# Joint classifier on one core: the logits load and the last store over two DMA queues, 64 partitions each, instead of SP's alone

## The chip, the cores and the metric

The kernel runs on one core of one Trainium2 chip. The metric is the device time of one execution in microseconds; the number given for a kernel is the median over its runs. A profile of one further execution of the kernel before is quoted below.

## The reference, cut to what matters

```python
# logits (512, 64), y_true (512, 100), float32
variables = [softmax(p, axis=-1) for p in split(logits, 4 parts of 16)]
joint = outer product of the four, per row        # (512, 16, 16, 16, 16)
flat = joint.reshape(B, -1)                       # (512, 65536)
num_y_joint = einsum('bj,by->yj', flat, y_true)   # summed over the rows
num_joint = sum(flat, axis=0)
prob_y_joint = clip(maximum(num_y_joint, 1e-6) / maximum(num_joint, 1e-6), 0, 1)
probs = einsum('yj,bj->by', prob_y_joint, flat)   # (512, 100)
```

Two large products over 65,536 joint states: one from rows to states (`num_y_joint`, with a column of ones beside the labels for `num_joint`), one back from states to rows (`probs`).

## The kernel before, in words

The 512 rows lie on 128 partitions, four (KC) to a partition. The four softmax variables are kept unnormalized; variables 2 and 3 make `p23`, variable 1 scales it into the tiles `p` (32 tiles of 128 states, fp16 in a high and a low part), variable 0 goes with the labels into `q` (four groups of four of its values). TensorE forms for each group and tile `numbers` = p^T q (`count`: twelve matmuls, three for each of the four chunks of rows), VectorE turns `numbers` into ratios (`make_ratios`), and TensorE sums `joined` = pt^T r (`join`: twelve matmuls), with `pt` the transposed `p`, made by DMA transposes of SP. There are 128 such steps. After each group ScalarE copies `joined` out (L271) and GpSimd scales and sums it into `acc`.

Each engine has its own instruction stream, in program order; the engines meet at semaphores only.

The start: SP issues the load of the logits into the tile `x` (L156, 128 partitions of 1 KB, semaphore `logits_in`), then the load of the labels (L157, `labels_in`). ScalarE's stream starts with the load of its function table, which the compiler has put ahead of the first Exp (both have line L217). VectorE waits for `logits_in` (L278), then takes the maxima of each variable (L279) and subtracts them (L283, two halves). ScalarE does the Exp of each half (L217). GpSimd makes the first part of `p23` (L186), ScalarE the first `p_hi` (L220), VectorE the first `qf` (L297, which reads the labels), ScalarE the first `q_hi` (L235), and TensorE's first matmul that counts is L481. Until then TensorE runs matmuls on a tile of zeros whose results are not used (`idle_turns`, L478): 14 from the moment the tile is set, 5 more once the first Exp is done (L491), 3 once `whole` is made (L493), 2 once the first `qf` is made (L495).

The end: the last matmuls (L636 to L638) leave the last 100 columns' sums of chunk 3 in two halves. VectorE adds the four last terms to `acc` (L421, `added`). SP stores chunks 0 to 2 of the result (L174, 150 KB) when their sums are complete, and the last chunk (L176, 128 partitions of 400 bytes) when `added` has reached 20. It then waits for both stores (`stored`, `stored_last`, L177 and L178).

Of the kernel before, what the change touches and what calls it, by code (L numbers as in the profile page):

```python
# [31 lines left out]
def joint_classifier(nc: bass.Bass, logits: bass.AP, y_true: bass.AP, probs: bass.AP):  # L32
    ROWS, WIDTH = logits.shape
    CLASSES = y_true.shape[1]
    LANES = 128
    KC = ROWS // LANES
    S = 16
    NV = WIDTH // S
    AG = 4
# [17 lines left out]
    with ctx:  # L57
        def sb(name, shape, dt):
            return ctx.enter_context(nc.sbuf_tensor(name, shape, dt))
# [4 lines left out]
        def sem(name):  # L64
            return ctx.enter_context(nc.semaphore(name))
# [7 lines left out]
        x = sb("x", [LANES, KC * NV, S], FP32)  # L73
# [25 lines left out]
        acc = sb("acc", [LANES, KC, CLASSES], FP32)  # L99
# [4 lines left out]
        logits_in = sem("logits_in")  # L104
# [31 lines left out]
        added = sem("added")  # L136
# [3 lines left out]
        stored_last = sem("stored_last")  # L140
# [6 lines left out]
        def landings(i):  # L147
            return (i // TURN_SEMS + 1) * 32 - (16 if i % TURN_SEMS == 0 else 0)

        def p_count(i):  # L150
            return KC + 2 if i == 0 else KC * (i + 1)


        @block.sync
        def _(sp):
            sp.dma_start(x[:, :, :], logits.rearrange("(p k) (v s) -> p (k v) s", k=KC, s=S)).then_inc(logits_in, 16)  # L156
            sp.dma_start(labels[:, :, 0:CLASSES], y_true.rearrange("(p k) y -> p k y", k=KC)).then_inc(labels_in, 16)  # L157

            def turn(out, src, i):
                return sp.dma_start_transpose(  # L160
                    out[:, i * 2 * TW:(i + 1) * 2 * TW].rearrange("p (c b) -> p c b", b=LANES),
                    src[:, i * 2 * TW:(i + 1) * 2 * TW])

            for i in range(S):
                landed = pt_landed[i % TURN_SEMS]
                if i >= TURN_SEMS:
                    sp.wait_ge(landed, landings(i - TURN_SEMS))
                sp.wait_ge(p_hi_made, p_count(i))
                turn(pt_hi, p_hi, i).then_inc(landed if i else first_landed, 16)
                sp.wait_ge(p_ready, p_count(i))  # L170
                turn(pt_lo, p_lo, i).then_inc(landed, 16)
            out = probs.rearrange("(p k) y -> p k y", k=KC)
            sp.wait_ge(added, KC * AG)
            sp.dma_start(out[:, 0:KC - 1, :], acc[:, 0:KC - 1, :]).then_inc(stored, 16)  # L174
            sp.wait_ge(added, KC * AG + AG)
            sp.dma_start(out[:, KC - 1:KC, :], acc[:, KC - 1:KC, :]).then_inc(stored_last, 16)  # L176
            sp.wait_ge(stored, 16)  # L177
            sp.wait_ge(stored_last, 16)  # L178

        @block.gpsimd  # L180
        def _(pool):
# [29 lines left out]

        @block.scalar
        def _(act):
            for part in range(2):
                v = NV // 2 * (1 - part)
                act.wait_ge(shifted, part + 1)
                act.activation(ek[:, :, v:v + NV // 2, :], ek[:, :, v:v + NV // 2, :], ACT.Exp).then_inc(exps, 1)  # L217

            def p_hi_chunk(i, k):
                return act.activation(p_hi[:, bass.ds(i * (2 * TW), 2 * TW)].rearrange("p (h k n) -> p h k n", h=2, k=KC)[:, :, k, :],  # L220
                                      p23[:, k, :].rearrange("p (h n) -> p h n", n=HALF),
                                      ACT.Copy, scale=v01s[:, k, 1, bass.ds(i, 1)])

            def first_p_hi(i, k):
                p_hi_chunk(i, k).then_inc(p_hi_made, 1)

            def make_p_hi(i):
                for k in range(KC):
                    last = p_hi_chunk(i, k)
                last.then_inc(p_hi_made, KC)  # L230

            def make_first_q_hi(part, k0, k1):

                act.wait_ge(q_made, part)
                act.activation(q_hi[:, k0 * NW:k1 * NW], qf[:, k0 * NW:k1 * NW], ACT.Copy).then_inc(q_hi_made, 1)  # L235

            def make_q_hi(g):

                for k in range(KC):
                    act.wait_ge(q_made, Q_PARTS + (g - 1) * KC + k + 1)  # L240
                    act.activation(q_hi[:, g * QW + k * NW:g * QW + (k + 1) * NW], qf[:, k * NW:(k + 1) * NW],
                                   ACT.Copy).then_inc(q_hi_made, 1)

            act.wait_ge(exps, 2)
            act.activation(v01s[:, :, :, :], ek[:, :, 0:2, :], ACT.Copy, scale=UP).then_inc(v01s_made, 1)
            act.wait_ge(v01s_made, 1)
            act.wait_ge(p23_first, 1)
            first_p_hi(0, 0)
            act.wait_ge(p23_first, 2)
            first_p_hi(0, 1)  # L250
            make_first_q_hi(1, 0, 1)
            first_p_hi(1, 0)
            make_first_q_hi(2, 1, 2)
            first_p_hi(1, 1)
            act.wait_ge(p23_made, 1)
            first_p_hi(0, 2)
            make_first_q_hi(3, 2, 3)
            first_p_hi(0, 3)
            make_first_q_hi(4, 3, 4)
            first_p_hi(1, 2)  # L260
            first_p_hi(1, 3)
            with act.Fori(2, S) as i:
                make_p_hi(i)

            for g in range(1, GROUPS):
                make_q_hi(g)
                if g > 1:
                    act.wait_ge(sum_chain, 3 * (g - 1) - 2)
                for k in range(KC):
                    act.wait_ge(joined_ready, (g - 1) * KC + (k + 1))  # L270
                    act.activation(left[:, k, :, :], joined[k][:, 0:PW].rearrange("p (a y) -> p a y", a=AG),  # L271
                                   ACT.Copy).then_inc(left_made, 1)

        @block.vector
        def _(dve):

            dve.memset(idle[:, :], 0.0).then_inc(idle_set, 1)
            dve.wait_ge(logits_in, 16)  # L278
            dve.tensor_reduce(stat[:, 0, :], x[:, :, :], AX.X, ALU.max).then_inc(dve_chain, 1)  # L279
            dve.wait_ge(dve_chain, 1)  # L280
            for part in range(2):
                v = NV // 2 * (1 - part)
# [381 lines left out]
```

## Time and profile before

| | us |
|---|---|
| median of 3 runs | 534.14 (534.1 to 534.17) |
| the profiled execution, its time | 534.18 |
| the profiled execution, its span from the first to the last instruction | 532.1 |

| engine | busy us | share of the span |
|---|---|---|
| PE (TensorE, matmul) | 527.9 | 99% |
| DVE (VectorE) | 295.9 | 56% |
| ACT (ScalarE) | 41.7 | 8% |
| POOL (GpSimd) | 24.0 | 5% |

The profile names engines PE, PEld (TensorE's weight load), DVE, ACT, POOL and SP; a q behind the name (SPq, ACTq) is that engine's instruction queue, where the issuing of DMAs and the waits are seen. L156 is line 156 of the kernel. Neighbouring matmuls overlap, so a matmul's own duration is longer than the distance to the next one.

### The profile page before, as it was taken

The numbers are of one execution on the slowest core, as the hardware profiler recorded it, in microseconds if no ns is written. First come the engines' busy times: TensorE is split into PE (matmuls) and PEld (weight loads), VectorE is DVE, ScalarE is ACT, GpSimd is POOL, SyncE is SP. The second block draws the span as 40 slices with busy tenths as digits, with TensorE's granted clock in tenths as the row PEclk, the third lists the DMA queues.
The fourth block names the chain that finished last, engine by engine and source line by source line (L and its number), as shares of the span: only waits on it lengthen the run. The fifth ranks groups of instructions, "written<-read, shape, count | busy, mean of one in ns | idle before, by whom it ended". The sixth has DMA issues, their size and how long they took to land.

```text
span 532.1 us, 8634 instructions
## 1 busy us (share of the span) xinstructions
PE 527.9 (99%) x3108; PEld 303.5 (57%) x3108; DVE 295.9 (56%) x764; ACT 41.7 (8%) x96; POOL 24.0 (5%) x22
## 2 busy tenths in 40 slices
PE   8999999999999999999999999999999999999997
PEld 5555555555555555555555555555555555555555
DVE  7986766754685444444466544444446544444446
ACT  7950000000200000000020000000001000000000
POOL 1000000000130000000032000000005000000000
PEclk9999999999999999999999999999999999999999
DMA  2944524220000000000000000000000000000000
GB/s 45 160 80 79 70 51 79 57 43 1 1 0 2 0 0 0 0 0 0 1 0 1 1 0 0 0 0 0 0 0 1 0 1 0 0 0 0 0 2 15
DMA packets 34770, 9.20 MB, mean 17 GB/s; under 512 B 34496, under 2 KB 34752, under 8 KB 34752
## 3 DMA queue, kind: packets, MB, share of 16 engines
q1 hardware_dynamic: 34752, 8.93, 9.4%
q8 instruction: 14, 0.23, 0.2%
q14 instruction: 4, 0.03, 0.0%
HBM read 0.34 MB, written 0.20 MB: 1 GB/s over the span
## 4 chain that ended last, share of the span: by engine, by line
PE 98%; DVE 1%; DMA 0%; ACT 0%; POOL 0%; issue 0%; ACTq 0%
PE joined L462 16%; PE joined L464 16%; PE joined L463 16%; PE numbers L454 16%; PE numbers L455 16%; PE numbers L456 16%; PE numbers L481 1%; PE numbers L484 1%; PE numbers L487 1%; DVE acc L421 0%; DMA x<-in_r_logits_dram 0%; ACT p_hi L220 0%; PE numbers L584 0%; PE numbers L581 0%; PE numbers L580 0%; PE joined L575 0%
## 5 line engine op out<-in xcount | busy, mean ns | idle before, releaser
L464 PE MATMUL joined<-r_hi,pt_lo 128*128 128x400 f16 x504 | 167.6, 332 | 0.0
L463 PE MATMUL joined<-r_lo,pt_hi 128*128 128x400 f16 x504 | 167.6, 332 | 0.0
L462 PE MATMUL joined<-r_hi,pt_hi 128*128 128x400 f16 x504 | 167.5, 332 | 0.0
L454 PE MATMUL numbers<-q_hi,p_hi 128*128 128x404 f16 x492 | 164.8, 335 | 0.0
L456 PE MATMUL numbers<-q_hi,p_lo 128*128 128x404 f16 x492 | 164.0, 333 | 0.0
L455 PE MATMUL numbers<-q_lo,p_hi 128*128 128x404 f16 x492 | 163.9, 333 | 0.0
L341 DVE TENSOR_SCALAR den<-numbers 128x4 f32<-128x4 f32 x128 | 20.6, 161 | 211.2 <-PE numbers L456 211.1
L353 DVE SCALAR_TENSOR_TENSOR r_lo<-ratio,r_hi 128x400 f16<-128x400 f32 x128 | 78.3, 612 | 4.4
L346 DVE SCALAR_TENSOR_TENSOR ratio<-numbers,inv 128x400 f32<-128x400 f32 x128 | 73.5, 574 | 4.4
L463 PEld LDWEIGHTS joined<-r_lo,pt_hi 128*128 (+1 forms) x504 | 49.2, 98 | 36.3
L462 PEld LDWEIGHTS joined<-r_hi,pt_hi 128*128 (+1 forms) x504 | 49.1, 97 | 36.3
L464 PEld LDWEIGHTS joined<-r_hi,pt_lo 128*128 (+1 forms) x504 | 49.3, 98 | 35.9
L455 PEld LDWEIGHTS numbers<-q_lo,p_hi 128*128 (+1 forms) x492 | 48.4, 98 | 35.8
L456 PEld LDWEIGHTS numbers<-q_hi,p_lo 128*128 (+1 forms) x492 | 47.6, 97 | 36.6
L454 PEld LDWEIGHTS numbers<-q_hi,p_hi 128*128 (+1 forms) x492 | 47.9, 97 | 35.9
L351 DVE TENSOR_SCALAR r_hi<-ratio 128x400 f16<-128x400 f32 x128 | 48.9, 382 | 4.4
L271 ACT ACTIVATE left<-joined 128x400 f32<-128x400 f32 x12 | 5.9, 504 | 317.7 <-PE joined L464 317.7
L321 DVE SCALAR_TENSOR_TENSOR p_lo<-p,v01s,p_hi 128x256 f16<-128x256 f32 x64 | 26.8, 478 | 0.0
L220 ACT ACTIVATE p_hi<-p,v01s 128x256 f32 (+1 forms) x64 | 26.1, 499 | 0.3 <-POOL p L186 0.3
L344 DVE RECIPROCAL inv<-den 128x4 f32<-128x4 f32 x128 | 22.8, 178 | 4.4
L199 POOL TENSOR_TENSOR part<-left,v0f 128x1600 f32<-128x1600 f32 x3 | 8.6, 2864 | 277.4 <-ACT left L271 277.4
L297 DVE SCALAR_TENSOR_TENSOR qf<-labels,whole,v01s 128x404 f32<-128x404 f32 x16 | 11.8, 734 | 0.0
(55 smaller groups left out, 84.7 us busy)
## 6 DMA issues: line engine op xcount, KB each, us to landing
pt_hi<-p_hi SPq DMA_TRANSPOSE x16, 3.1
pt_lo<-p_lo SPq DMA_TRANSPOSE x16, 3.2
labels<-in_r_y_true_dram SPq DMA_DIRECT2D x1, 200.0 KB, 2.9
out_dram<-acc SPq DMA_DIRECT2D x1, 150.0 KB, 1.8
x<-in_r_logits_dram SPq DMA_DIRECT2D x1, 128.0 KB, 2.0
out_dram<-acc SPq DMA_DIRECT2D x1, 50.0 KB, 1.5
```

The costliest lines, as they stand in the source:

```text
L220: return act.activation(p_hi[:, bass.ds(i * (2 * TW), 2 * TW)].rearrange("p (h k n) -> p h k n", h=2, k=KC)[:, :, k, :], p23[:, k, :].rear ...
L321: return dve.scalar_tensor_tensor(lo[:, :, k, :], p23[:, k, :].rearrange("p (h n) -> p h n", n=HALF), v01s[:, k, 1, bass.ds(i, 1)], hi[:, ...
L344: dve.reciprocal(inv[:, slot, :], den[:, slot, :]).then_inc(inv_made, 1)
L346: dve.scalar_tensor_tensor(ratio[:, slot, :].rearrange("p (a y) -> p a y", a=AG), got[:, :, 0:CLASSES], STABLE, inv[:, slot, :].unsqueeze( ...
L351: dve.tensor_scalar(r_hi[:, r_slot, :], ratio[:, slot, :], UP, 0.0, ALU.min, ALU.max).then_inc(r_hi_made, 1)
L353: dve.scalar_tensor_tensor(r_lo[:, r_slot, :], ratio[:, slot, :], UP, r_hi[:, r_slot, :], ALU.min, ALU.subtract).then_inc(ratios_ready, 1)
L454: pe.matmul(out, p_at(p_hi, tile, k), q_at(q_hi, g, k), start=(k == 0), stop=False)
L455: pe.matmul(out, p_at(p_hi, tile, k), q_at(q_lo, g, k), start=False, stop=False)
L456: last = pe.matmul(out, p_at(p_lo, tile, k), q_at(q_hi, g, k), start=False, stop=(k == KC - 1))
L462: pe.matmul(out, p_at(pt_hi, tile, k), r_hi[:, slot, :], start=first, stop=False)
L463: pe.matmul(out, p_at(pt_hi, tile, k), r_lo[:, slot, :], start=False, stop=False)
L464: last = pe.matmul(out, p_at(pt_lo, tile, k), r_hi[:, slot, :], start=False, stop=final)
```

## The change

The load of the logits is cut into two DMAs: SP issues the one for partitions 0 to 63, ScalarE, as the first thing in its stream as written, the one for partitions 64 to 127. Both count on `logits_in`, and VectorE waits for 32 instead of 16. The store of the last chunk is cut in the same way: SP stores partitions 0 to 63; ScalarE, at the end of its stream, waits for the same count of `added` and stores partitions 64 to 127. SP's last wait is for 32 on `stored_last`.

```diff
         @block.sync
-            sp.dma_start(x[:, :, :], logits.rearrange("(p k) (v s) -> p (k v) s", k=KC, s=S)).then_inc(logits_in, 16)
+            rows = logits.rearrange("(p k) (v s) -> p (k v) s", k=KC, s=S)
+            sp.dma_start(x[0:LANES // 2, :, :], rows[0:LANES // 2, :, :]).then_inc(logits_in, 16)
...
             sp.wait_ge(added, KC * AG + AG)
-            sp.dma_start(out[:, KC - 1:KC, :], acc[:, KC - 1:KC, :]).then_inc(stored_last, 16)
+            sp.dma_start(out[0:LANES // 2, KC - 1:KC, :], acc[0:LANES // 2, KC - 1:KC, :]).then_inc(stored_last, 16)
             sp.wait_ge(stored, 16)
-            sp.wait_ge(stored_last, 16)
+            sp.wait_ge(stored_last, 32)
...
         @block.scalar
+            rows = logits.rearrange("(p k) (v s) -> p (k v) s", k=KC, s=S)
+            act.dma_start(x[LANES // 2:LANES, :, :], rows[LANES // 2:LANES, :, :]).then_inc(logits_in, 16)
...
+            out = probs.rearrange("(p k) y -> p k y", k=KC)
+            act.wait_ge(added, KC * AG + AG)
+            act.dma_start(out[LANES // 2:LANES, KC - 1:KC, :], acc[LANES // 2:LANES, KC - 1:KC, :]).then_inc(stored_last, 16)
 
         @block.vector
-            dve.wait_ge(logits_in, 16)
+            dve.wait_ge(logits_in, 32)
```

## Rows read from the trace of the kernel before

**Rows 1.** The page: the chain of waits that ended last, shares by engine.
```profile
PE 98%; DVE 1%; DMA 0%; ACT 0%; POOL 0%; issue 0%; ACTq 0%
```

**Rows 2.** Everything PE waited for: us in total, times, longest.
```profile
PE numbers L478 <- DVE idle L277: 1.0, 1, 1.0
PE numbers L481 <- ACT q_hi L235: 0.3, 1, 0.3
```

**Rows 3.** The chain in order of time at the start: start us, us, what.
```profile
0.72 2.05 DMA x<-in_r_logits_dram
2.76 0.02 issue
2.79 0.43 DVE stat L279
...
3.24 0.30 DVE x L283
...
3.56 0.32 ACT x L217
...
3.95 0.63 POOL p L186
...
5.69 0.48 ACT q_hi L235
6.17 0.14 issue
6.30 0.50 PE numbers L481 x2
```

**Rows 4.** The chain's last piece at the end.
```profile
529.76 0.32 DVE acc L421
```

**Rows 5.** Instructions in order, start: start us, us, engine, line, operation [idle before].
```profile
0.72 0.38 SPq L156 DMA_DIRECT2D x<-in_r_logits_dram  x1
0.72 1.28 ACT L217 ACT_TABLE_LOAD   x1 [0.72 <-PEq L652]
...
1.16 0.65 SPq L157 DMA_DIRECT2D labels<-in_r_y_true_dram  x1
...
3.56 0.51 ACT L217 ACTIVATE x<-x 128x128 f32<-128x128 f32 x2 [1.56 <-DVE x L283]
...
4.84 0.74 DVE L297 SCALAR_TENSOR_TENSOR qf<-labels,whole,v01s 128x404 f32<-128x404 f32 x1
```

**Rows 6.** The same view of SP's queue at the end.
```profile
528.68 0.36 SPq L174 DMA_DIRECT2D out_dram<-acc  x1
530.11 0.33 SPq L176 DMA_DIRECT2D out_dram<-acc  x1
```

**Rows 7.** DMA issues: KB each, us from issue to landing.
```profile
labels<-in_r_y_true_dram SPq DMA_DIRECT2D x1, 200.0 KB, 2.9
out_dram<-acc SPq DMA_DIRECT2D x1, 150.0 KB, 1.8
x<-in_r_logits_dram SPq DMA_DIRECT2D x1, 128.0 KB, 2.0
out_dram<-acc SPq DMA_DIRECT2D x1, 50.0 KB, 1.5
```

**Rows 8.** DMA traffic from 0 to 6 us in 40 slices of 0.15.
```profile
GB/s 0 0 0 0 0 0 0 0 0 0 0 34 239 232 287 82 0 56 139 155 277 323 280 118 19 0 0 0 0 0 0 0 0 0 0 0 0 0 0 0
```

**Rows 9.** The same from 528 to 532 us, slices of 0.1.
```profile
GB/s 0 0 0 0 0 0 0 0 0 0 0 0 0 0 0 96 336 360 348 300 96 0 0 0 0 0 0 0 0 80 268 152 12 0 0 0 0 0 0 0
```

**Rows 10.** PE's idle-turn matmuls, four short windows: start us, us to the last one's end.
```profile
4.00 0.63 PE L478 MATMUL numbers<-idle 128*128 128x256 f16 x2
...
4.21 0.63 PE L478 MATMUL numbers<-idle 128*128 128x256 f16 x2
...
5.21 0.83 PE L478 MATMUL numbers<-idle 128*128 128x256 f16 x4
...
5.32 0.27 PE L478 MATMUL numbers<-idle 128*128 128x256 f16 x1
```

**Rows 11.** Windows: us, PE busy (x), PEclk (granted clock, 1.00 is full), DMA share, GB/s.
```profile
3.00:4.00 1.00, 1.00 (x6) 1.00 0.59 152
```

**Rows 12.** Whom SP's queue waited for: us in total, times, longest.
```profile
SPq L178 <- DMA out_dram<-acc: 1.2, 1, 1.2
```

## The prediction

> **What bounds the kernel now.** I read the chain of waits first. It is TensorE for 98% of the span, and no DMA has a share that rounds to 1% [rows 1]. The view of PE's waits says where TensorE can still be moved: it waits twice in the whole execution, 1.0 us before its first idle matmul and 0.3 us for the first `q_hi` [rows 2]. So from 6.30 us to its end it never stands still. The time is thus three pieces: what leads to 6.30, a block of matmuls that the change doesn't touch, and a tail behind the last matmul. The change touches the first piece and the last.
>
> The chain in order of time shows the first piece: the logits' DMA is out from 0.72 for 2.05 us, and then maxima, subtraction, Exp, `p23`, `p_hi` and `q_hi` follow one another to the first L481 at 6.30 [rows 3]. Each tenth that `x` lands earlier or later moves all this, and with it the whole kernel, by a tenth. The last piece: the last L421 ends at 529.76 + 0.32 = 530.08 [rows 4], SP issues the last store at 530.11 [rows 6], it lands 1.5 us later [rows 7], at 531.6, and the span ends at 532.1.
>
> The sum is made against the profiled execution: 534.18 us, which is its span of 532.1 and 2.1 around it. The median of the runs is 534.14, so 0.04 is all that lies between them.
>
> **The load, piece by piece.** Of the 2.0 us from issue to landing [rows 7], the traffic takes the slices from 1.65 to 2.4, most of it between 1.75 and 2.35 [rows 8]. So about 1.0 us passes before the first byte, 0.6 us moves 128 KB, and 0.4 us (2.35 to 2.76) passes until VectorE is released. Only the middle part depends on the amount. The two halves together are the same 128 KB. What can shrink: SP's issue, 0.38 us for 128 partitions [rows 5]. The last store issues 50 KB in 0.33, the one before it 150 KB, three times as many rows, in 0.36 [rows 6]: between these, issue time hardly depends on how much is issued, and half the partitions save at most 0.02. Bounds of the load:
> - Gain: the first byte comes 0.8 us behind the issue, as in the last store (530.11 to the slice at 530.9) [rows 6, 9], instead of 1.0, and two queues fill the 0.6 us of traffic better, to half of it. That is 0.2 + 0.3 = 0.5 us. The rate in it is 232 to 287 GB/s, and the 150 KB store runs at 336 to 360 [rows 8, 9], so there is some room, though not for twice.
> - Loss: the two issues, which now start together at 0.72, go one behind the other, 0.38 us later for the second half.
> The row nearest to it is that of the same load, 2.0 us, and VectorE is released by the later of two landings, which is rather late than early. I take +0.05.
>
> **Labels.** L157 now starts some hundredths earlier or at the same 1.16. It lands at 1.16 + 2.9 = 4.06 [rows 5, 7], and L297 reads it at 4.84: 0.78 us of cover. Its traffic starts at about 2.55, when that of `x` is over [rows 8]. If ScalarE's half came 0.38 late, the two would overlap and share the engines; the labels' cover stays larger than that. Cost 0; without the cover each tenth would count, since `qf` stands ahead of the first `q_hi`.
>
> **ScalarE's start.** Its stream has the function table's load at 0.72 for 1.28 us, and then nothing until the Exp at 3.56, an idle time of 1.56 [rows 5]. The compiler put the load ahead of the Exp. The new DMA is written ahead of both. It adds 0.38 and the 0.06 to the next instruction (SP's 0.72 + 0.38 to 1.16), so the load runs from 1.16 to 2.44, and 1.12 us of the idle time is left. Cost 0. Behind the load wait only the Exps, which VectorE releases later anyway.
> That the load stays behind the DMA is supported by the Trainium skill, "ScalarE: Activation LUTs", What happens when an exp ACTIVATE runs, by which the load is placed right before the ACTIVATE that needs it. The same page, in What ACT_TABLE_LOAD costs, gives 1283 ns for the load, and the row's 1.28 agrees, but also a drain of some 1380 ns behind it, which no row here shows. By that page ScalarE would be ready at 2.44 + 1.38 = 3.82 instead of 3.56, and the kernel 0.26 later.
>
> **The last store.** 50 KB: first byte 0.8 us behind the issue, traffic in the slices from 530.9 to 531.3, landing at 531.6 [rows 6, 7, 9]. ScalarE has had nothing to do since it copied the third group's `joined` out, so its wait for `added` costs nothing, and nothing is queued behind its DMA. SP's only work behind its half is its wait, 1.2 us now [rows 12]. Gain at most half of the traffic, 0.17; loss at most one issue behind the other, 0.33. The DMAs of both ends are issued at the same moment, so I take +0.03, again for the later of two. L174's 150 KB are over by 530.1 [rows 9] and are not met.
>
> **Sum.** 534.18 + 0.05 + 0.03 = 534.26; less the 0.04 to the median, some 534.2. The bounds alone give 534.14 - 0.5 - 0.17 = 533.5 and 534.14 + 0.38 + 0.33 = 534.85.
>
> A rule of the Trainium skill speaks against the change: "DMA: Bandwidth & Descriptors", Rules for kernel authors, advises against two transfers to disjoint halves of the partitions, since both run over the same 16 DMA engines; its section Issuing engines are not separate DMA queues leaves only the issuer's time to be saved. By it the traffic's halving above would be 0, and no gain over 0.02 at either end would be left.
>
> **The rivals.**
> 1. Two queues overlap well. For it: the load's 232 to 287 GB/s against 360 in the store. Against: the same engines carry both. Say two thirds of the bounds: 0.33 + 0.11, giving 533.7.
> 2. One behind the other: the issues of SP and ScalarE, or what makes descriptors behind them, take turns. For it: no row has two queues at once, so nothing excludes it. Time 534.85. If the half of `x` is over 0.12 late, this meets a further step, which makes rival 3.
> 3. Slower, by TensorE's clock. The idle matmuls (256 columns) start every 0.21 us at 4.00 and 4.21, which is the 1.2 GHz level, and 0.11 apart at 5.21 and 5.32, the 2.4 GHz level; the profile's granted clock reads 1.00 in both [rows 10, 11]. TensorE had run without a gap since 1.04 when that came. The fifteenth starts at 4.00 and waits for the Exp, done at 3.88 [rows 3, 10]: from `x` being 0.12 later, a gap opens there. If the rise then comes later than the first real matmul, each matmul until it takes 0.17 longer; ten of them are 1.7 us. With `x` 0.38 late and the tail 0.33 late: 534.14 + 0.71 + 1.7 = 536.5. Against: `x` must be late at all, and 1.1 us lie between the rise and 6.30.
> 4. The table's load ends up ahead of the DMA (it needs no operand and could be put at the head of the stream). ScalarE's half is then issued at 2.00 instead of 0.72, and all behind `x` comes 1.28 later: 535.4, before what the gap at 4.00 adds.
> 5. The load stays behind the DMA, but ScalarE isn't ready right after it. The trace shows only that it was within 1.56 us. If all of that were needed, the Exp is later by the shift of 0.44: 534.6. By the page's drain it is 534.4, as above.
>
> **How the numbers follow.** The forecast (both ends within 0.15 us of now) has 0.56; rival 1 0.12; rival 2 0.15; rival 3 0.04; rival 4 0.06; rival 5 0.06. One in a hundred is left for something faster by over 1 us, which no bound here reaches. A measurement tells a change from none at about 0.2%, 1.07 us: the forecast and rivals 1, 2 and 5 lie within it, 0.89; rivals 3 and 4 are slower, 0.10; faster 0.01. The range goes from rival 1 to a little above rival 2: 533.7 to 534.9; the forecast's own is 533.9 to 534.5.
>
> **What would show it right or wrong.** L279 starting between 2.6 and 2.95; ScalarE's DMA row at 0.72 ahead of the table's load; the first L481 at 6.30 moved by what L279 moved, and nothing else waiting in PE's waits; both last stores issued at 530.1 plus that shift, landing within 1.4 to 1.7. It is wrong if the load row stands first, if L279 starts over 0.3 later, if idle matmuls at 0.21 spacing reach up to the first L481, if the labels' L297 starts to wait for a DMA, or if the part of the time outside the span (2.1 us) changes with a second queue in use.

## The result and the profile after

| | before | after |
|---|---|---|
| median of 22 runs, us | 534.11 (533.98 to 534.29) | 534.85 (534.78 to 535.13) |
| profiled execution: time, span | 534.18, 532.1 | 534.88, 533.1 |

The ratio is 1.0014 (95% interval 1.0008 to 1.002): the change costs 0.74 us. That is below the 0.2% by which the chances were given, but every run after is slower than every run before.

The chain of waits of the kernel after, at the start (start us, us, what), is the answer to [rows 3]:

```profile
0.72 2.49 DMA x<-in_r_logits_dram
3.21 0.02 issue
3.24 0.43 DVE stat L285
...
3.69 0.30 DVE x L289
...
4.02 0.32 ACT x L220
...
6.14 0.47 ACT q_hi L238
6.62 0.14 issue
6.75 0.50 PE numbers L487 x2
```

The first real matmul starts at 6.75 instead of 6.30. Of these 0.45 us, 0.44 are in the DMA's row, 2.49 instead of 2.05; each piece behind it has its old length.

Instructions in order in the kernel after, at the start and at the end, against [rows 5, 6]:

```profile
0.72 0.57 SPq L157 DMA_DIRECT2D x<-in_r_logits_dram  x1
0.72 0.58 ACTq L216 DMA_DIRECT2D x<-in_r_logits_dram  x1
...
1.33 1.28 ACT L220 ACT_TABLE_LOAD   x1 [1.33 <-PEq L658]
1.34 0.60 SPq L158 DMA_DIRECT2D labels<-in_r_y_true_dram  x1
...
4.02 0.51 ACT L220 ACTIVATE x<-x 128x128 f32<-128x128 f32 x2 [1.40 <-DVE x L289]
...
5.30 0.73 DVE L303 SCALAR_TENSOR_TENSOR qf<-labels,whole,v01s 128x404 f32<-128x404 f32 x1
...
530.55 0.55 SPq L177 DMA_DIRECT2D out_dram<-acc  x1
530.56 0.53 ACTq L278 DMA_DIRECT2D out_dram<-acc  x1
```

All four halves take 0.53 to 0.58 us to issue; the undivided DMAs took 0.38 and 0.33. The time to landing, in the list of DMA issues, against [rows 7]:

```profile
labels<-in_r_y_true_dram SPq DMA_DIRECT2D x1, 200.0 KB, 3.2
out_dram<-acc SPq DMA_DIRECT2D x1, 150.0 KB, 1.8
x<-in_r_logits_dram SPq DMA_DIRECT2D x1, 64.0 KB, 2.2
x<-in_r_logits_dram ACTq DMA_DIRECT2D x1, 64.0 KB, 2.5
out_dram<-acc SPq DMA_DIRECT2D x1, 25.0 KB, 1.9
out_dram<-acc ACTq DMA_DIRECT2D x1, 25.0 KB, 2.1
```

Half of the bytes lands later than the whole did: 2.2 and 2.5 against 2.0, 1.9 and 2.1 against 1.5. Each DMA counts its semaphore up by sixteen, and both halves count on the same one. The list gives the first sixteen counts to the row that was issued first and the last sixteen to the other, whichever DMA they came from. So the smaller number of a pair says only that neither half was complete before it. The larger one is sure: it is when both are complete, which is what the kernel waits for.

The traffic from 0 to 6 us shows when the bytes go, beside [rows 8]:

```profile
GB/s 0 0 0 0 0 0 0 0 0 0 0 0 0 20 123 280 246 109 148 154 93 165 237 235 232 125 56 16 0 0 0 0 0 0 0 0 0 0 0 0
```

It sets in at 1.95 us instead of 1.65, though SP and ScalarE issue at 0.72 as SP did before. Counted by queue (q1 is SP's, q10 ScalarE's: packets, MB, share of 16 engines), the two tenths from 2.2 and from 2.5 us read:

```profile
q1 hardware_dynamic: 18, 0.02, 57.5%
...
q10 hardware_dynamic: 20, 0.02, 50.3%
q1 hardware_dynamic: 2, 0.00, 1.1%
```

So at the load the halves hardly run side by side. SP's half comes first, from 2.06 to 2.54, and ScalarE's follows it, from 2.33 to 2.92. At the store it is otherwise. The tenths from 531.8 and from 531.9 us by queue:

```profile
q10 hardware_dynamic: 30, 0.01, 47.2%
q1 hardware_dynamic: 19, 0.01, 27.2%
...
q1 hardware_dynamic: 43, 0.01, 56.0%
q10 hardware_dynamic: 34, 0.01, 40.9%
```

Here both halves move at once, ScalarE's first packet at 531.76 and SP's at 531.80, and the pair still is complete only 2.1 us after its issue.

Two more things moved. The span grew by 1.0 us, the time only by 0.7. And TensorE met a short gap, new among its waits [rows 2]:

```profile
PE numbers L484 <- DVE idle L283: 1.0, 1, 1.0
PE numbers L487 <- ACT q_hi L238: 0.3, 1, 0.3
PE numbers L484 <- ACT x L220: 0.2, 1, 0.2
```

### The profile page after: what moved, and what is told of

The parts are those of the page before. It is cut to its first block, busy times and chain, and to the rows that moved or that the text cites. A ratio compares the mean times of both kernels' runs of the same rounds, so it can differ in the third digit from the quotient of the medians.

```text
span 533.1 us, 8636 instructions
## 1 busy us (share of the span) xinstructions
PE 528.3 (99%) x3108; PEld 303.3 (57%) x3108; DVE 295.8 (55%) x764; ACT 41.7 (8%) x96; POOL 24.0 (5%) x22
## 4 chain that ended last, share of the span: by engine, by line
PE 98%; DVE 1%; DMA 0%; ACT 0%; POOL 0%; issue 0%; ACTq 0%
PE joined L468 16%; PE joined L470 16%; PE joined L469 16%; PE numbers L460 16%; PE numbers L461 16%; PE numbers L462 16%; PE numbers L487 1%; PE numbers L490 1%; PE numbers L493 1%; DVE acc L427 0%; DMA x<-in_r_logits_dram 0%; ACT p_hi L223 0%; PE numbers L590 0%; PE numbers L587 0%; PE numbers L586 0%; PE joined L581 0%
```

## The experiments

Three theories were put up. Theory 1: two engines that issue at the same moment slow each other. Theory 2: a DMA of 64 partitions is slower, whoever issues it. Theory 3: ScalarE's queue is slow. Each experiment is the kernel before with the edit shown; where two DMAs count on one semaphore, the wait on it goes from 16 to 32, which the cuts below leave out. Differences are against runs of the kernel before on the same chip; "mean span" is over the runs of a kernel, and that of the kernel before is 532.14 to 532.18 in each group. Most of the times' intervals are about 0.5 us wide to either side, so several of them include 1 (no difference). The mean spans part the kernels more finely: each comes from 11 runs or more, and the spans of one kernel mostly lie within 0.4 us.

**One end at a time.** e1_load_only has the change's load, e2_store_only its last store.

```diff
# e1_load_only
-            sp.dma_start(x[:, :, :], ...)
+            sp.dma_start(x[0:LANES // 2, :, :], rows[0:LANES // 2, :, :]).then_inc(logits_in, 16)
+            act.dma_start(x[LANES // 2:LANES, :, :], rows[LANES // 2:LANES, :, :]).then_inc(logits_in, 16)
# e2_store_only
-            sp.dma_start(out[:, KC - 1:KC, :], acc[:, KC - 1:KC, :]).then_inc(stored_last, 16)
+            sp.dma_start(out[0:LANES // 2, KC - 1:KC, :], ...)
+            act.dma_start(out[LANES // 2:LANES, KC - 1:KC, :], ...)   # after act.wait_ge(added, ...)
```

> Only the load of the logits is split, the last store is as before. The changed kernel's trace has the first L487 0.45 us later than before and the rest of its 0.74 at the end. If the two ends simply add, this is 534.11 + 0.45 = 534.56, with both issues at 0.57 us and the first real matmul at 6.75. Rival: the time between the runs' figure and the span (2.1 before, 1.8 after) belongs to the start, then it is some 534.3.

> Only the last store is split, the load is as before. If the two ends add: 534.11 + 0.74 - 0.45 = 534.40, while the span grows by about 0.55 us, because the store's halves land 1.9 and 2.1 us after their issue instead of 1.5; then 0.25 of the span's growth is not in the time. If that part belongs to the start: 534.65. First real matmul at 6.30.

Measured: e1 534.57 against 534.22 (ratio 1.0007, 0.9998 to 1.0016), mean span 532.53, +0.35. e2 534.83 (1.0012, 1.0003 to 1.0021), mean span 532.76, +0.58. The spans add up: 0.35 + 0.58 = 0.93, and the kernel after has 533.06, +0.88 (against 532.18, the e1 and e2 group's). The times don't: 0.35 + 0.61 = 0.96 against 0.74, so the expectation of 534.40 for e2 failed, and its rival's 534.65 too; e1's 534.56 came. e1's interval includes 1, but only the slowest of 33 runs before (534.52) reaches its fastest (534.49). Outside the span e1 and e2 have 2.05 us each, as before (2.0), and only both together have 1.81. The store is the larger part. In e1's trace ScalarE's half came first, the other way round than after; the tenths from 2.1 and from 2.4 us by queue:

```profile
q10 hardware_dynamic: 23, 0.02, 118.1%
...
q1 hardware_dynamic: 17, 0.02, 69.1%
q10 hardware_dynamic: 1, 0.00, 0.6%
```

Neither queue has precedence. The list of issues still gives SP's half 2.2 and ScalarE's 2.5 here, though ScalarE's went first, which shows how little the smaller number says.

**Who issues, and how many at once.** e3 issues both halves from SP. e4 is the kernel before with an unused load of 64 partitions on ScalarE at the start; SP waits for it (`spare_in`) at its very end.

```diff
# e3_load_halves_sp
+            sp.dma_start(x[0:LANES // 2, :, :], rows[0:LANES // 2, :, :]).then_inc(logits_in, 16)
+            sp.dma_start(x[LANES // 2:LANES, :, :], rows[LANES // 2:LANES, :, :]).then_inc(logits_in, 16)
# e4_extra_act_load
+            act.dma_start(spare[:, :, :], rows[LANES // 2:LANES, :, :]).then_inc(spare_in, 16)
```

> Both halves of the load are issued by SP, one behind the other, then the labels; the store is as before. Theory 1 (two engines that issue at the same moment slow each other): each half's issue takes 0.38 us or less, as the whole did, the second starts at 1.16 and lands at about 3.1; time 534.11 + 0.35 to 0.45 = 534.5. Theory 2 (a DMA of 64 partitions is slower to issue, whoever issues it): each takes 0.57, the second starts at 1.35 and lands at about 3.5: 534.9. Theory 3 (ScalarE's queue is slow): issue 0.38 each, as theory 1; the trace of the next kernel parts the two.

> The kernel before, with one more DMA: ScalarE loads 64 rows of the logits into a tile that nothing reads, at the start. SP's load of all 128 partitions is as before. Theory 1: SP's issue of the load goes from 0.38 to about 0.57, its landing is late by 0.2 to 0.4 us, and the time is 534.3 to 534.5 although no result waits for ScalarE's DMA. Theories 2 and 3: SP's issue stays at 0.38 and the landing at 2.0; time 534.1, or 534.2 if the extra 64 KB are moved before x's last bytes.

Measured: e3 534.88 (1.0016, 1.0007 to 1.0025), e4 534.2 against 534.22. SP's and ScalarE's queues in order in e3's trace, and then in e4's:

```profile
0.72 0.58 SPq L157 DMA_DIRECT2D x<-in_r_logits_dram  x1
...
1.35 0.57 SPq L158 DMA_DIRECT2D x<-in_r_logits_dram  x1
```

```profile
0.71 0.39 SPq L158 DMA_DIRECT2D x<-in_r_logits_dram  x1
0.72 0.54 ACTq L218 DMA_DIRECT2D spare<-in_r_logits_dram  x1
```

This parts the theories. In e3 SP issues alone and still takes 0.58 and 0.57. In e4 it issues all 128 partitions while ScalarE issues 64, and takes its usual 0.39. The long issue goes with the DMA of 64 partitions and not with the company. Theory 1 is wrong for the issue's length, theory 2 stands. In e4's trace `x` lands after 2.1 us instead of 2.0, as it does in e2's and e7's, which have no second DMA at the start.

**ScalarE's queue by itself.** e5 moves the last store whole to ScalarE, e6 moves both loads there, e8 lets ScalarE wait at its end and issue nothing.

```diff
# e5_store_act_alone (SP's own last store goes)
+            act.dma_start(out[:, KC - 1:KC, :], acc[:, KC - 1:KC, :]).then_inc(stored_last, 16)
# e6_loads_act (SP's loads go)
+            act.dma_start(x[:, :, :], ...).then_inc(logits_in, 16)
+            act.dma_start(labels[:, :, 0:CLASSES], ...).then_inc(labels_in, 16)
# e8_act_waits_only
+            act.wait_ge(added, KC * AG + AG)
```

> The last chunk's store is issued whole by ScalarE and by it alone; SP only waits for it. Load as before. Theory 1 (issuing at the same moment is what costs): issue 0.33 and landing 1.5 us, as on SP: 534.1. Theory 3 (ScalarE's queue is slow): issue 0.55, landing 2.0: 534.4 to 534.6.

> Logits and labels are both loaded whole over ScalarE's queue, in the old order, and SP issues nothing at the start. The function table's load comes behind both, at about 1.8 to 3.1 us, ahead of the Exp at 3.56. Theory 1: issue 0.38, landing 2.0, time 534.1. Theory 3: issue 0.57, landing 2.5, time 534.5.

> The kernel before, with ScalarE waiting for the last sum at the end of its stream and issuing nothing. If ScalarE's late end is what lies between the span's growth and the time's (span +1.0, time +0.7), the time here falls below that of before by up to 0.25 us at the same span, or the span grows and the time doesn't. If that difference comes with the second DMA queue, nothing changes: 534.11 and span 532.1.

Measured: e5 534.12 against 534.21 (1.0, 0.9991 to 1.0009), issue 0.38, landing 1.6. e6 533.96 (0.9996, 0.9987 to 1.0005), issue 0.40, mean span 532.20, no shorter than before's 532.17. Its profiled execution, one of its two longest (534.21), has a landing of 2.2 instead of the expected 2.0. e8 534.16. ScalarE's queue costs about what SP's does, so theory 3 is wrong. ScalarE's late end (e8) does nothing to the part outside the span either.

**The store's halves apart in time.** In e7 SP waits for the 150 KB store before it issues its half.

```diff
# e7_store_staggered
+            sp.wait_ge(stored, 16)
             sp.dma_start(out[0:LANES // 2, KC - 1:KC, :], ...)
```

> The last store is split over the two queues, but SP issues its half only when the 150 KB store has landed, about 530.5, after ScalarE's issue is over. Load as before. Theory 1: each half issues in 0.33 us and lands 1.5 after its own issue, the last at 532.0 against 531.6: time 534.1 plus 0 to 0.4, and the span 532.5. Theory 2: each issues in 0.55 and lands 1.9 to 2.1 later: span 533.0.

Measured: 534.81 (1.0013, 1.0004 to 1.0022), mean span 532.86. Both queues in its trace, with the list of landings below:

```profile
530.15 0.55 ACTq L275 DMA_DIRECT2D out_dram<-acc  x1
530.59 0.54 SPq L177 DMA_DIRECT2D out_dram<-acc  x1
```

```profile
out_dram<-acc ACTq DMA_DIRECT2D x1, 25.0 KB, 1.8
out_dram<-acc SPq DMA_DIRECT2D x1, 25.0 KB, 1.8
```

The issues overlap by 0.1 us only, and each still takes about 0.55. The packets don't meet at all (ScalarE's from 531.35 to 531.62, SP's from 531.78 to 532.05), so here both landings can be trusted. Both are 1.8 us, where in e2, issued together, the pair is complete after 2.1. So there are two costs: 0.3 us for the 64 partitions (1.5 to 1.8), and 0.3 more for a second DMA at the same moment (1.8 to 2.1).

Where they lie can be read from the packets and the counts of `stored_last` in the traces. The 64 partitions cost time ahead of the first packet: it comes 1.2 us behind the issue in e7, and 0.83 behind the whole store's in the kernel before. The second DMA costs in more than one way. In e2 its packets begin when the first one's end (531.40 and 531.67). In the kernel after the packets run together, over by 532.12, but the 32 counts come one by one until 532.63, 0.51 us behind the last packet. In the kernel before the last of 16 counts comes 0.39 us behind it (531.64 and 531.25).

**Two queues without halved partitions.** Half of the bytes on each queue, but all 128 partitions in each DMA, so that the two DMAs together have twice the packets.

```diff
# e9_load_by_rows
+            sp.dma_start(x[:, 0:KC * NV // 2, :], rows[:, 0:KC * NV // 2, :]).then_inc(logits_in, 16)
+            act.dma_start(x[:, KC * NV // 2:KC * NV, :], rows[:, KC * NV // 2:KC * NV, :]).then_inc(logits_in, 16)
# e10_store_by_classes
+            sp.dma_start(out[:, KC - 1:KC, 0:CLASSES // 2], ...)
+            act.dma_start(out[:, KC - 1:KC, CLASSES // 2:CLASSES], ...)
```

> The load of the logits goes over SP's and ScalarE's queues, half of the bytes each, but cut by rows of the data and not by partitions: each DMA has all 128 partitions, 512 bytes apiece. Store as before. Theory 2 (a DMA of 64 partitions is slower to issue): both issue in about 0.4 us, x lands 2.0 to 2.3 us after 0.72, time 534.2 to 534.4, against 534.57 for the halves of partitions. If it is the second queue and not the partitions: issue 0.55 and 534.57.

> The last store goes over both queues, half of the bytes each, cut by classes: each DMA has all 128 partitions, 200 bytes apiece. Load as before. Theory 2: both issue in about 0.35 us and land 1.5 to 1.8 later: 534.2 to 534.5. If it is the two queues at one moment: 534.8, as with the halves of partitions.

Measured: e9 534.18 against 534.13 (1.0001, 0.9992 to 1.0011), mean span 532.20, +0.06. e10 534.43 (1.0006, 0.9997 to 1.0015), mean span 532.49, +0.36. The list of issues in e10, where the second cost stands alone:

```profile
out_dram<-acc SPq DMA_DIRECT2D x1, 25.0 KB, 1.5
out_dram<-acc ACTq DMA_DIRECT2D x1, 25.0 KB, 1.8
```

The first sixteen counts are in when the whole DMA's were, the last sixteen 0.3 later. At the store, then, 0.36 of the 0.58 is the second queue and about 0.2 the 64 partitions. At the load nearly all of the 0.35 comes with the cut by partitions: there the pair is complete after 2.0 us in e9, as the whole load was. How much of it is the number 64, the next experiment shows. e10's interval includes 1, but none of its 11 spans (532.3 to 532.9) is below the longest of the 20 before (532.3).

**Which partition counts.** ScalarE's stream is idle from about 405 us on. e11 lets it issue a series of loads into an unused tile there, each waiting for the one before; e12 has another series in another order, and at the start a load split into 96 and 32 partitions.

```diff
# e11_partition_counts (and with other counts e12_load_96_32)
+            act.dma_start(spare[0:128, :, :], rows[0:128, :, :]).then_inc(spare_in, 16)
+            act.wait_ge(spare_in, 16)
+            act.dma_start(spare[0:64, :, :], rows[0:64, :, :]).then_inc(spare_in, 16)
+            act.wait_ge(spare_in, 32)
...
# e12_load_96_32, at the start
+            sp.dma_start(x[0:96, :, :], rows[0:96, :, :]).then_inc(logits_in, 16)
+            act.dma_start(x[96:LANES, :, :], rows[96:LANES, :, :]).then_inc(logits_in, 16)
```

> The kernel before, and at the end of ScalarE's stream, where it has nothing to do for over 100 us, eight loads into an unused tile, each waiting for the one before: partitions 0-127, 0-63, 64-127, 0-31, 0-95, 0-15, 0-111 with 1 KB each, then 0-127 with 512 bytes. Theory 2 as a threshold (only all 128 partitions are quick): 0.38 us to issue for the first and the last, 0.54 to 0.58 for the six others, with landings 0.2 to 0.3 us later than size alone would give. Theory 2 as a cost of the half alone: 0.55 for 64 partitions only. Rival: none shows the difference when alone on an idle queue, so that it comes from what else is issued at the start and the end: all 0.33 to 0.40. Time as before, 534.1.

> Two things that don't meet in time. (a) The load of the logits is split over the two queues by partitions, but 96 on SP and 32 on ScalarE; store as before. (b) At the end of ScalarE's stream the series of loads into an unused tile again, in another order: partitions 0-95, 0-63, 0-127, 64-127, 0-31, then 0-63 with 512 bytes, 0-47, 0-79. If 64 partitions are what is slow to issue: (a) both issues at 0.40 or less, time 534.2 to 534.3 against 534.57 for 64 and 64; (b) 0.47 to 0.55 for the three 64s wherever they stand, 0.32 to 0.40 for all others. If in the first series the order made it (the first DMAs slow, later ones quick) or any split of partitions is slow at the cold start: (b) the first one or two slow, whatever their size, the third 64 as quick as the rest; (a) 0.55 and 534.5 to 534.6.

ScalarE's queue in e12's trace. The partitions are, in order, 0-95, 0-63, 0-127, 64-127, 0-31, 0-63 with 512 bytes, 0-47, 0-79:

```profile
405.24 0.34 ACTq L278 DMA_DIRECT2D spare<-in_r_logits_dram  x1
407.61 0.52 ACTq L280 DMA_DIRECT2D spare<-in_r_logits_dram  x1
409.79 0.36 ACTq L282 DMA_DIRECT2D spare<-in_r_logits_dram  x1
411.75 0.47 ACTq L284 DMA_DIRECT2D spare<-in_r_logits_dram  x1
413.98 0.32 ACTq L286 DMA_DIRECT2D spare<-in_r_logits_dram  x1
415.62 0.48 ACTq L288 DMA_DIRECT2D spare<-in_r_logits_dram  x1
417.54 0.32 ACTq L290 DMA_DIRECT2D spare<-in_r_logits_dram  x1
419.39 0.32 ACTq L292 DMA_DIRECT2D spare<-in_r_logits_dram  x1
```

The three DMAs of 64 partitions take 0.47 to 0.52, wherever they stand and whatever their bytes; the five others take 0.32 to 0.36. e11 reads the same: 0.39 for 128, 0.52 and 0.47 for the two 64s, then 0.35, 0.32, 0.32, 0.32 for 32, 96, 16 and 112, and 0.35 for 128 with 512 bytes. It ran once, in 533.95 us. So "only all 128 are quick" is wrong. Of the eight counts tried, 64 alone is slow. To landing, 64 KB over 64 partitions take 2.2 us in e12, 80 KB over 80 partitions 1.9. (The first load of each series lands late whatever its count, after 2.5 us for 128 partitions in e11 and 2.4 for 96 in e12, and is left out of this comparison.)

At e12's start the issues are 0.39 and 0.41, as expected. Its time is 534.15 against 534.2 (1.0, 0.9991 to 1.0009), but its mean span is 532.38, +0.21, between e9's +0.06 and e1's +0.35. Its profiled execution, the longest of its spans (532.6), even has the pair complete after 2.5 us and the first real matmul at 6.75, like the kernel after. Its first packet comes at 1.74, as before, but the packets then take until 2.74, where the whole load's were over by 2.42. So three cuts of the load over two queues cost three amounts: +0.06 with whole partitions, +0.21 at 96 and 32, +0.35 at 64 and 64. Between 96 and 32 and 64 and 64 lie 0.14 of e1's 0.35 (the long issues, by the theory, though e12's parts are uneven too). Another 0.15 comes with a cut by partitions even where the issues are short, and what makes it is not shown. The store was not tried at 96 and 32. At neither end is a cut over two queues faster than one queue.

## Why the prediction came out as it did

The time lies in the stated range (533.7 to 534.9), on its upper edge, and "within 0.2%" was the likeliest outcome. The forecast of 534.2 and its own range up to 534.5 missed: of the 0.74 us its terms held 0.08. Two of its own signs of being wrong came: the maxima (L279, now L285) started 0.45 us later, over the 0.3 allowed, and the part outside the span went from 2.1 to 1.8. The last stores were complete after 2.1 us, outside its 1.4 to 1.7. So the range held, but the mechanism behind the two terms did not.

- **Where the change acts.** Right. A later landing of `x` went through to the first matmul one to one (0.45 and 0.45), and from there to the last L427, which ends at 530.21 + 0.32 = 530.53 instead of 530.08. The block between didn't change.
- **"Half the partitions save at most 0.02" of the issue.** This is the step that failed. It was read off two stores, both of 128 partitions, which differ in bytes and rows; nothing in the trace had 64. Both were also made of 128 packets, one to a partition. The same rows held a warning: the labels' load, 128 partitions too but 400-byte packets, four to a partition, took 0.65 to issue [rows 5], so the issue does depend on more than the partitions' number. Half the partitions don't save 0.02, they add 0.2 us to each issue, and about 0.3 to the store's landing (e7: 1.8 against 1.5).
- **The load, +0.05.** Measured +0.45 in the profiled execution, +0.35 as e1's mean. The lower bound, that two queues fill the traffic better, was never approached: the queues' packets came for the most part one behind the other, over 0.86 us (2.06 to 2.92) where the whole load's took 0.67. The loss bound of 0.38 was about the right size, but for another reason: the issues, which it put one behind the other, ran at the same time.
- **The store, +0.03, loss bound 0.33.** Measured +0.58 (e2). The bound was exceeded, since it held only the second queue (0.36 by e10) and not the partitions (the other 0.2).
- **Rival 2, one behind the other.** Its 534.85 is the measured median, but by luck of the sum. It supposed that the second issue would wait for the first, 0.38 at the start. The issues overlap fully; what comes in turn is most of the load's traffic, and beside it stands a cost the rival hadn't. The third term is the part outside the span, some 0.2 us less, that it didn't know either.
- **Rival 3, TensorE's clock.** Its gap came (0.17 us ahead of L484), and the 2.4 GHz level came later: the idle matmuls after are still 0.22 us apart at 5.63, where before they were 0.11 apart from 5.21 [rows 10]:

```profile
5.63 0.64 PE L484 MATMUL numbers<-idle 128*128 128x256 f16 x2
...
5.85 0.54 PE L484 MATMUL numbers<-idle 128*128 128x256 f16 x2
```

  But it came before the first real matmul: those at 6.75 and 6.92 start 0.17 us apart, as the first two did before (6.30 and 6.47), so nothing was paid. e3's trace, whose gap was 0.47 us, shows the same. The granted clock reads 1.00 throughout in these traces. In one run of e3 the rival may have come true. It took 536.54 us against 534.7 to 535.07 in its ten others, its granted clock was 0.997 where theirs was 1.0, and the 1.7 us between are the size that rival 3 worked out. It wasn't profiled, so this isn't shown.
- **Rivals 4 and 5, the function table.** Neither came: the DMA stands first, the load runs from 1.33 to 2.61, and the Exp waits for VectorE. The 1380 ns of drain of the Trainium skill ("ScalarE: Activation LUTs", What ACT_TABLE_LOAD costs) would have it ready at 3.99, just before the 4.02 at which it started, so the trace after can't tell. ScalarE's rows of e6 can:

```profile
1.80 1.28 ACT L217 ACT_TABLE_LOAD   x1 [1.80 <-issue]
...
3.74 0.51 ACT L217 ACTIVATE x<-x 128x128 f32<-128x128 f32 x2 [0.66 <-DVE x L283]
```

  The load ends at 3.08 and the Exp starts 0.66 later, when VectorE releases it, and not at 4.46. The drain isn't paid here; the measurement decides.
- **Labels.** Right: by the list landed at 4.54, read at 5.30.
- **The Trainium skill's advice** against disjoint halves of the partitions ("DMA: Bandwidth & Descriptors", Rules for kernel authors) held, and for more than its reason. By it there is nothing to gain. The runs show a loss of 0.74, part of it from the 64 partitions as such.

## What to carry to other kernels

A small DMA on the critical path is nearly all fixed time (here 1.4 of 2.0 us), so halving its bytes can save little, and a second DMA adds another fixed time. A bound on an issue's cost has to come from a row with the same shape, the partition count included; size alone is not the shape. If a transfer has to be cut over two queues, cut it along the free dimension and keep the partitions whole (e9 against e1: +0.06 against +0.35; e10 against e2: +0.36 against +0.58, so that even this isn't free). Where two DMAs count on one semaphore, only the time at which both are complete can be read from it.

## What the runs showed of the hardware that was not expected

- DMAs of 64 partitions issue in 0.47 to 0.58 us on SP and on ScalarE, loads and stores, alone and in company. Those of 16, 32, 48, 80, 96, 112 and 128 partitions, with one packet to a partition, issue in 0.32 to 0.41. The labels' load, with four packets to each of 128 partitions, takes 0.59 to 0.83. Why 64 is different stays open.
- Of two DMAs of like size issued at the same moment on the two queues, the first packets came 0.27 us apart in e1, in e2 and at the load of the kernel after, 0.18 in e9, 0.11 in e10, and only 0.04 at the store of the kernel after. Either queue can be first.
- The part of the time outside the span is 1.75 to 1.81 us in the four kernels with two or more DMAs on ScalarE's queue (after, e6, e11 with its single run, e12) and 1.95 to 2.05 in the ten others, with one or none. These 0.2 us are about what lies between the span's 0.88 and the time's 0.74. Their cause was not found; e8 shows that it isn't ScalarE's late end.
